# Attention kernel with three rotating max banks, masks of single-head diagonal tiles on VectorE, and the unit loop written out

## The reference

```python
Q, K, V = (split_heads(x @ W.T) for W in (Wq, Wk, Wv))      # [4, 16, 1024, 16]
Q, K = rope(Q), rope(K)
logits = einsum('bhnd,bhmd->bhnm', Q, K) / sqrt(16)
logits = where(causal, logits, -inf)
probs = softmax(logits, axis=-1)
attn = einsum('bhnm,bhmd->bhnd', probs, V)
```

## Time and profile before

| | us |
|---|---|
| median of 3 runs | 1235.57 |
| lowest and highest run | 1234.23, 1236.41 |
| the profiled execution's own time | 1237.32 |
| its span, first to last instruction | 1235.6 |
| TensorE matmul busy | 1099.6 (89%) |
| VectorE busy | 705.3 (57%) |
| ScalarE busy | 478.9 (39%) |
| GpSimd busy | 335.9 (27%) |

### The profile page before, as it was taken

One profiled execution on the slowest core, in us unless ns is written; L12 is line 12 of the kernel. 1 busy time (PEld: TensorE's weight loads), 2 busy tenths in 40 slices (PEclk: granted clock), 3 DMA queues, 4 the chain that ended last, 5 costly groups with the idle time before them and its releaser, 6 DMA issues. The chain is left out here.

```text
span 1235.6 us, 19774 instructions
## 1 busy us (share of the span) xinstructions
PE 1099.6 (89%) x5906; PEld 571.6 (46%) x5906; DVE 705.3 (57%) x1452; ACT 478.9 (39%) x719; POOL 335.9 (27%) x478
## 2 busy tenths in 40 slices
PE   8990899999999999999983699999997799999995
PEld 4550234444443444444422466666664455555553
DVE  5992878888888888888811344554453133333332
ACT  2441046666666666666671222222222122222221
POOL 2335022222222222222221122322335322322332
PEclk9995589999999999999997699999999799999998
DMA  7657334444455455455007322212012212222211
GB/s 263 148 135 152 51 57 61 80 93 80 64 93 89 60 93 94 60 94 94 10 14 216 104 60 61 64 58 69 35 36 80 78 54 64 61 66 66 65 62 39
DMA packets 78253, 99.76 MB, mean 81 GB/s; under 512 B 28048, under 2 KB 64400, under 8 KB 74864
## 3 DMA queue, kind: packets, MB, share of 16 engines
q1 hardware_dynamic: 67568, 74.41, 29.3%
q0 software_dynamic: 5712, 15.93, 3.5%
q10 hardware_dynamic: 4912, 8.66, 2.3%
HBM read 65.86 MB, written 32.70 MB: 80 GB/s over the span
## 5 line engine op out<-in xcount | busy, mean ns | idle before, releaser
L592 DVE TENSOR_REDUCE maxima<-max_ps 128x1 f32<-128x512 f32 (+3 forms) x608 | 384.7, 660 | 114.6 <-PE max_ps L448 61.4
L539 ACT ACTIVATE probs<-scores_ps 128x1024 f32<-128x1024 f32 (+3 forms) x384 | 290.4, 809 | 160.0 <-PE scores_ps L468 158.5
L444 PE MATMUL max_ps<-k_stack,q_stack 96*128 96x512 bf16 (+3 forms) x768 | 248.7, 346 | 43.4 <-DMA q_stack<-q_parts 32.8
L468 PE MATMUL scores_ps<-q_stack,k_stack 99*128 99x512 bf16 (+3 forms) x768 | 182.9, 327 | 2.0 <-ACT probs L539 1.8
L676 POOL TENSOR_SCALAR_AFFINE_SELECT probs<-probs 128x512 f32<-128x512 f32 x128 | 81.2, 635 | 374.4 <-ACT probs L539 374.4
L444 PEld LDWEIGHTS max_ps<-k_stack,q_stack 96*128 96x128 bf16 x768 | 74.7, 98 | 233.2 <-DVE maxima L592 174.0
L488 PE MATMUL out_ps<-probs,v_ones 128*32 128x512 f32 (+3 forms) x1536 | 164.0, 499 | 4.0 <-POOL probs L676 1.8
L1087 ACT ACTIVATE silu<-gate_ps 128x512 f32<-128x512 f32 x71 | 42.4, 597 | 253.2 <-PE gate_ps L980 145.1
L1235 DVE TENSOR_TENSOR hidden<-silu,up_ps 128x512 f32<-128x512 f32 x71 | 48.7, 686 | 160.4 <-PE up_ps L990 105.4
L448 PE MATMUL max_ps<-mask,ident_bf 128*128 128x128 bf16 x512 | 104.8, 229 | 0.0
L999 PE MATMUL down_ps<-v_then_down,hidden_t 128*128 x312 | 79.1, 397 | 10.5 <-issue 9.7
(11 more groups left out here) (142 smaller groups left out, 1178.7 us busy)
## 6 DMA issues: line engine op xcount, KB each, us to landing
k_stack<-k_parts SPq DMA_DIRECT2D x96, 128.0 KB, 4.5
q_stack<-q_parts SPq DMA_DIRECT2D x96, 128.0 KB, 7.5
q_parts<-parts SPq DMA_DIRECT2D x32, 192.0 KB, 3.2
k_parts<-parts SPq DMA_DIRECT2D x32, 192.0 KB, 3.1
rows_in<-expert_rows SPq DMA_DIRECT2D x39, 136.0 KB, 2.1
sums_in<-expert_sums SPq DMA_DIRECT2D x39, 128.0 KB, 2.0
x_t<-in_x_cols SPq DMA_DIRECT2D x8, 512.0 KB, 11.2
heads_rows<-heads_out SPq DMA_DIRECT2D x32, 128.0 KB, 3.6
```

Source lines behind the costliest of these rows:

```text
L444: last = nc.tensor.matmul(bank, q_stack[:ROWS, u.slot, h0 + k, t * P:(t + 1) * P], k_stack[:ROWS, u.slot, h0 + k, chunk * BLOCK:chunk * BL ...
L468: last = nc.tensor.matmul(scores_ps[:, pair, k, n0:], k_stack[:ROWS_MAX, u.slot, h, mt * P:(mt + 1) * P], q_stack[:ROWS_MAX, u.slot, h, c ...
L539: nc.scalar.activation(probs[:, s % RING, 2 * pair:2 * pair + 2, n0:], scores_ps[:, pair, :, n0:], ACT.Exp).then_inc(exp_done, 1)
L592: nc.vector.tensor_reduce(maxima[:, u.slot, chunk, h0:h0 + heads, t], max_ps[:, n % 2, :heads * keys].rearrange("p (h k) -> p h k", h=head ...
```

## The change

The four parts of it, all in the attention stage:

- `max_ps` gets a third bank, the one that was `turn_ps`. Pieces, output transposes and the transpose of the maxima all take their bank in turn from one list (`bank_plan`), and TensorE waits for whoever had the bank three turns before. VectorE's normalise moves from steps 3 and 7 to steps 2 and 6.
- In the 16 single-head diagonal pieces the mask matmul is left out. VectorE instead runs one instruction that adds a float32 mask of 512 columns (`mask_wide`, in SBUF) to the tile and takes the maximum, and that also writes the sum to a scratch tile in bfloat16. Before it VectorE waits for its own piece n-3 and issues an event instruction (`stand`). Pieces with two and four heads keep the mask matmuls.
- GpSimd makes `mask_wide` at the start of the stage, ahead of its other constants, and VectorE waits for it once.
- `each_unit` writes out all 16 units. All waits get constant values.

```diff
-def each_unit(eng, step):
-
-    for i in range(2):
-        step(Unit.number(i))
-    with eng.Fori(0, (UNITS - 4) // Unit.RING) as turn:
-        for k in range(2, 2 + Unit.RING):
-            step(Unit(turn * Unit.RING + k, k % Unit.RING, turn + k // Unit.RING))
-    for i in range(UNITS - 2, UNITS):
+def each_unit(step):
+
+    for i in range(UNITS):
         step(Unit.number(i))
...
+def bank_plan(pieces, places, early):
...
+    users = [("piece", 0, n) for n in range(len(pieces))]
+    users += [("piece", 1, n) for n in range(2)] + [("max", 0, 0)] + [("piece", 1, n) for n in range(2, early)]
+    for u in range(UNITS):
+        for s in range(len(places) // 3):
+            if s == 2 and u:
+                users.append(("out", u - 1, 1))
+            if s == 6:
+                users.append(("out", u, 0))
+            if s == 9 and u + 1 < UNITS:
+                users.append(("max", u + 1, 0))
+            of = u + (1 if s < OWN_STEPS else 2)
+            for slot in range(3 * s, 3 * s + 3):
+                users += [("piece", of, n) for n in places[slot] if of < UNITS]
+    users.append(("out", UNITS - 1, 1))
+    return {user: at for at, user in enumerate(users)}, users
...
+        mask_wide = b.sb("mask_wide", [P, BLOCK])
+        masked_out = b.sb("masked_out", [P, 6, BLOCK], BF16)
         scores_ps = b.ps("scores_ps", [P, 2, 2, BLOCK])
-        max_ps = b.ps("max_ps", [P, 2, BLOCK])
+        max_ps = b.ps("max_ps", [P, BANKS, BLOCK])
         out_ps = b.ps("out_ps", [P, BLOCK])
-        turn_ps = b.ps("turn_ps2", [P, BT, P])
+
+        def bank(kind, u, n):
+            return max_ps[:, turn_at[kind, u, n] % BANKS]
...
+            def bank_free(kind, u, n):
+
+                at = turn_at[kind, u, n] - BANKS
+                if at < 0:
+                    return
+                kind, u, n = users[at]
+                if kind == "piece":
+                    pe.wait_ge(piece_reduced, PIECES * u + n + 1)
+                elif kind == "max":
+                    pe.wait_ge(neg_copied, u + 1)
+                else:
+                    pe.wait_ge(normed, 2 * u + n + 1)
...
-                    wait(pe, piece_reduced, PIECES * u.i + n - 1)
+                    bank_free("piece", u.i, n)
                     for k in range(heads):
-                        bank = max_ps[:, n % 2, k * keys:(k + 1) * keys]
-                        diagonal = chunk == t // BT
-                        last = nc.tensor.matmul(bank, q_stack[:ROWS, u.slot, h0 + k, t * P:(t + 1) * P],
+                        part = bank("piece", u.i, n)[:, k * keys:(k + 1) * keys]
+                        diagonal = chunk == t // BT and heads > 1
+                        last = nc.tensor.matmul(part, q_stack[:ROWS, u.slot, h0 + k, t * P:(t + 1) * P],
...
                 pe.wait_ge(combined, u.i + 1)
-                wait(pe, normed, 2 * u.i - 1)
-                nc.tensor.transpose(turn_ps[:GROUP * SEQ_TILES, 0],
+                bank_free("max", u.i, 0)
+                nc.tensor.transpose(bank("max", u.i, 0)[:GROUP * SEQ_TILES, :P],
...
                 pe.wait_ge(out_copied, 2 * u.i + c + 1)
-                wait(pe, normed, 2 * u.i + c)
-                if c == 1:
-                    wait_neg = u.ahead(1)
-                    if wait_neg.exists():
-                        pe.wait_ge(neg_copied, wait_neg.i + 1)
+                bank_free("out", u.i, c)
...
                     dve.wait_ge(piece_done, PIECES * u.i + n + 1)
+                    if chunk == t // BT and heads == 1:
+                        wait(dve, piece_reduced, PIECES * u.i + n - 3)
+                        stand(dve, dve_stood)
+                        nc.vector.tensor_tensor_reduce(
+                            masked_out[:, n % 6, :keys], bank("piece", u.i, n)[:, :keys], mask_wide[:, BLOCK - keys:], 1.0,
+                            NEG, ALU.add, ALU.max, maxima[:, u.slot, chunk, h0:h0 + 1, t]).then_inc(piece_reduced, 1)
+                        continue
...
-                    if s == 3:
+                    if s == 2:
                         normalise(u.ahead(-1), 1)
-                    if s == 7:
+                    if s == 6:
                         normalise(u, 0)
...
+            dve.wait_ge(wide_made, 1)
             reduce(Unit.number(0), range(PIECES))
...
+            nc.gpsimd.memset(mask_wide[:], 0.0).then_inc(consts_half, 1)
+            pool.wait_ge(consts_half, 2)
+            tail = mask_wide[:, BLOCK - P:]
+            nc.gpsimd.affine_select(out=tail, in_=tail, compare_op=ALU.is_ge, fill=NEG, base=0,
+                                    pattern=[[-1, P]], channel_multiplier=1).then_inc(wide_made, 1)
```

More of the change, by code:

```diff
@@ L349, in attend @@
     STEPS, PIECES = len(steps), len(pieces)
+    BANKS = 3
+    turn_at, users = bank_plan(pieces, places, EARLY)
     DIAGONAL = [s for s, (c, mt, _) in enumerate(steps) if mt >= BT * c]
@@ L383, in attend @@
         heads_stored = [b.sem("heads_stored0"), b.sem("heads_stored1")]
-        pool_stood = b.sem("pool_stood")
+        pool_stood, dve_stood, wide_made = b.sem("pool_stood"), b.sem("dve_stood_a"), b.sem("wide_made")
         block = ctx.enter_context(nc.Block())
@@ L423, in _ @@
             send_neg(Unit.number(0))
-            each_unit(sp, step)
+            each_unit(step)
             store_heads(Unit.number(UNITS - 1), 1)
@@ L447, in find_max @@
                         if diagonal:
-                            last = nc.tensor.matmul(bank[:, keys - P:], ident_bf[:], mask[:],
+                            last = nc.tensor.matmul(part[:, keys - P:], ident_bf[:], mask[:],
                                                     start=False, stop=True)
@@ L495, in turn_out @@
                 pe.wait_ge(out_copied, 2 * u.i + c + 1)
-                wait(pe, normed, 2 * u.i + c)
-                if c == 1:
-                    wait_neg = u.ahead(1)
-                    if wait_neg.exists():
-                        pe.wait_ge(neg_copied, wait_neg.i + 1)
+                bank_free("out", u.i, c)
                 for t in range(BT):
-                    last = nc.tensor.transpose(turn_ps[:, t], out_t[:, c, t * P:(t + 1) * P], ident[:])
+                    last = nc.tensor.transpose(bank("out", u.i, c)[:, t * P:(t + 1) * P], out_t[:, c, t * P:(t + 1) * P], ident[:])
                 last.then_inc(out_turned, 1)
@@ L527, in _ @@
             pe.wait_ge(k_ones, 1)
-            each_unit(pe, step)
+            each_unit(step)
             times_v(Unit.number(UNITS - 1), STEPS - 1)
@@ L553, in negate @@
                 wait(act, neg_split, 4 * u.i)
-                nc.scalar.mul(neg_max[:], turn_ps[:GROUP * SEQ_TILES, 0], -1.0).then_inc(neg_copied, 1)
+                nc.scalar.mul(neg_max[:], bank("max", u.i, 0)[:GROUP * SEQ_TILES, :P], -1.0).then_inc(neg_copied, 1)
             def load_weights(u):
-                if isinstance(u.i, int) or u.slot == 1:
+                if not 2 <= u.i < UNITS - 2 or u.slot == 1:
                     return
@@ L578, in _ @@
             negate(Unit.number(0))
-            each_unit(act, step)
+            each_unit(step)
             copy_out(Unit.number(UNITS - 1), 1)
@@ L591, in reduce @@
                     dve.wait_ge(piece_done, PIECES * u.i + n + 1)
+                    if chunk == t // BT and heads == 1:
[5 more added lines that the diff above has]
+                        continue
                     nc.vector.tensor_reduce(maxima[:, u.slot, chunk, h0:h0 + heads, t],
-                                            max_ps[:, n % 2, :heads * keys].rearrange("p (h k) -> p h k", h=heads),
+                                            bank("piece", u.i, n)[:, :heads * keys].rearrange("p (h k) -> p h k", h=heads),
                                             X, ALU.max).then_inc(piece_reduced, 1)
@@ L609, in normalise @@
                 wait(dve, heads_stored[c], 16 * u.i)
-                rows = turn_ps[:].rearrange("p t (h e) -> p t h e", h=GROUP)
+                rows = bank("out", u.i, c).rearrange("p (t h e) -> p t h e", t=BT, h=GROUP)
                 nc.vector.reciprocal(recip[:, c], rows[:, :, :, DK]).then_inc(recip_done, 1)
@@ L630, in _ @@
             reduce(Unit.number(1), range(EARLY))
-            each_unit(dve, step)
+            each_unit(step)
             normalise(Unit.number(UNITS - 1), 1)
@@ L690, in _ @@
             split_neg(Unit.number(0))
-            each_unit(pool, step)
+            each_unit(step)
 def by_batch(eng, step):
```

## The result

The changed kernel takes 1184.4 us in the median of four runs (1182.9 to 1186.2), the one before 1235.3: a ratio of 0.9587 (95% interval 0.9572 to 0.9602). In a second series of runs it took 1187.2 us, against 1236.2 for the one before (ratio 0.9598, 0.9581 to 0.9615). So 49 to 51 us are gone, about 4.1%. The forecast was 37.5 off, 1198, with 1190 as its lower end: the direction and the place were right, the size was not.

What follows compares the result with a forecast made beforehand. TensorE was taken to bound the attention units, with stalls on two banks. 15 x (0.96 masks + 1.4 third bank) = 35.4, plus 0.6 loop and 1.5 start, gave 37.5 us off: 1198 us, range 1190 to 1225.

Steps and rivals of the forecast that it cites:

- What bounds it: Attention units: TensorE sets the 31.3 us period, 29.6 us streaming, switching or awaiting inputs plus 1.7 us waiting for banks.
- Mask matmuls: TensorE in attention units: leaving out 16 single-head mask matmuls of 0.06 us saves 0.96 us a unit.
- The new instruction: VectorE in attention units: 16 adds with a maximum raise its work from 23.2 to 25.6 us; TensorE stays the bound.
- x: Cost of VectorE's add with a maximum above a plain reduce: taken as 0.15 us, bounds 0.08 and 0.6.
- below 0.1 us of latency where it waits: VectorE's queue: assumed delay from the added event instruction and its wait when VectorE is not behind.
- The third bank: TensorE's bank waits in attention units: 1.7 us removed less 0.3 left for lateness, saving 1.4 us a unit.
- reserve for a late combine: End of each attention unit: 0.3 us held back because VectorE's combine could come up to 0.6 us later.
- The start: Before the first exp: 51 pieces gain 0.10 us each, 5.1, less 3.6 for 24 new instructions: 1.5 us saved.
- The loop: Attention unit loop written out: 12 units times 0.05 us, 0.6 us saved; jump-fetch stalls of microseconds dismissed.
- The sum: Whole kernel: 35.4 over 15 periods, 0.6 and 1.5 make 37.5 us off, 1198 us as a median.
- The signs: Expected attention traces: period 28.6 to 29.1 us, VectorE busy some 26.5, new instruction 0.68 to 0.85, reduces every 0.60.
- VectorE as the bound at x = 0.4: Rival in attention units: VectorE needs 30.1 us a unit, about 14 us off, 1222 us; chance 0.13.

Runs made afterwards that it cites:

- u_banks: Kernel before with the unit loop written out and three rotating banks, transposes included, but all 32 mask matmuls and plain reduces kept: 1199.5 us.
- u_masks: Kernel before with the unit loop written out and the 16 single-head masks added on VectorE, still two max banks and separate transpose bank: 1240.7 us.
- masks_wait_first: u_masks with VectorE's wait on its own third last piece and the event instruction moved ahead of the wait for the tile: 1227.0 us.
- fill_015: Kernel after with an 80-column reduce ahead of each new VectorE instruction, about 0.15 us more for each: 1201.2 us.
- loop_after: Kernel after with units 2 to 13 put back in the hardware loop on all engines: 1200.6 us.
- fill_040: Kernel after with a 320-column reduce ahead of each new VectorE instruction, about 0.40 us more for each: 1252.9 us.
- loop_vector_alone: Kernel after with units 2 to 13 in the hardware loop on VectorE only, all other engines written out: 1199.6 us.
- four_heads: Kernel after with the two four-head pieces of a unit also masked on VectorE, by an add into SBUF and then a reduce: 1181.2 us.

## Why the prediction was wrong

- **What bounds it** was right: TensorE streams in the attention units and stalls on two banks. My count of nine stalls and 1.7 us a unit was short: u_banks got 1.94 us a unit back.
- **Mask matmuls**, 0.96 us a unit: right (0.92), but only with the third bank. I added the parts as if each held alone. With two banks the part is a loss of 6 us (u_masks), or half its worth with the waits put first (masks_wait_first).
- **The new instruction**, x = 0.15: this term and what hung on it are the step that failed. It measured 0.01. My lower bound, 0.08, was a small instruction's price put on top; but the accumulator read of 0.08 us is recorded at the very start of the next instruction (228.42 and 229.03), so it does not push it back. The Trainium skill was right that there are two instructions ("VectorE: DVE Perf Modes", Two Vector instructions with no wait between them), and the trace shows both; it says nothing of a price, and there is nearly none. The term "below 0.1 us of latency where it waits" measured 0.17 (u_masks), hidden in the kernel after.
- **The third bank**, 1.4 us a unit: too low by 0.54, of which 0.24 is the count above and 0.3 the reserve for a late combine, which at the real x was not needed. At the x that I assumed the reserve itself was too small: fill_015, with x at about 0.16, loses 0.8 us a unit, and takes 1201.2 us, near the forecast of 1198, with the short reserve on one side and the short count and the start on the other.
- **The start**, 1.5 us: measured 6.8. The step of 0.10 us a piece was right (0.70 to 0.60); the 3.6 us taken off for x were nearly all not there (24 x 0.01 = 0.2). The rest: gaps between groups of reduces, 0.2 to 0.3 us each, were not in the sum and are mostly gone, and pieces of 384 columns, priced as 512, follow each other at 0.47 us where VectorE has no gap (126.21 to 126.68). So a piece fell by 0.13 us in the mean, not by 0.10.
- **The loop**, 0.6 us: right for the kernel before. My dismissal of the Trainium skill's rule on jumps ("Runtime: NRT & Kernel Launch", Instruction fetch mechanics: a taken branch whose target is not in the loaded pages waits for a fetch) was right for its rows and wrong for the change: with the masks on VectorE the loop would have cost three gaps of 4.7 to 5.8 us, and the trace agrees with the rule there, with a fetched packet in each gap. Writing it out is worth 13 to 16 us there (loop_after against the two series of the kernel after).
- **The sum.** 15 x 0.54 + 5.3 = 13.4 on top of 37.5 is 50.9, less 0.6 for the masks (0.92 in place of 0.96) 50.3; measured 49.0 to 49.7 in the spans. Of the 13.4, 7.9 hang on x (the reserve, 4.5, and 3.4 at the start): with x = 0.01 the prediction's own sum is 45.4 off, 1190, the very end of the range. The other 5.5, the short count of the bank waits (3.6) and the rest of the start (1.9), put the result outside it. The lower end was the sum at x = 0.08 with the counted stalls and 2 us for the last stage: its unknown price was bounded, though not low enough, its counts were not.
- **The signs.** Max tiles without waits for one another, 0.22 to 0.23 us from a tile of 512 columns to the next tile or scores, the new instruction at 0.69 us and unit 0's reduces every 0.60 came as said. The period, 28.37, and VectorE's 24.5 us a unit lie below the 28.6 to 29.1 and the 26.5 that were named, the one by the short count (31.3 - 0.96 - 1.94 is 28.4), the other by x.
- **The rivals.** The third bank does pay. VectorE as the bound at x = 0.4 was priced at 1222 and measured 1252.9 (fill_040): VectorE's work alone, plus 0.5, does not give the period, which is 2.6 us longer than that work. TensorE then waits 17.0 + 11.2 us in 12 units for the combine; how much of the 2.6 is that and how much the depth of three banks was not separated. The prediction's count of 264 new instructions is 8 too high, since 8 of the 24 at the start belong to unit 1, which is among the 15: the kernel has 256.

## What to carry to other kernels

The waits of a two-deep rotation are a cycle of latencies, so whatever takes work off one engine but starts later on the other can lose (here 6 us); deepen the rotation first, then move the work, and value each part with the other in place. Put waits that are always met, and event instructions, ahead of the wait that is not. Before an engine's stream is made longer inside a hardware loop, check that its turn of the loop still runs without a gap at the jump back; where the profile says "issue" for some microseconds once a turn, write that engine's stream out.

## What the hardware showed that was not expected

- In the loop of the kernel before VectorE's instruction stream stays loaded, and a unit with a jump back in it is no longer than the others (31.29 us in the mean, 31.24 written out). The longer stream of the kernel after stands 4.7 to 5.8 us at each jump, for VectorE alone (loop_after, loop_vector_alone), and is fetched again in every turn. How long a stream may be was not tried.
- An add with a maximum over 128x512 in PSUM and SBUF costs 0.61 us back to back, the plain reduce 0.60, accumulator read included.
- A wait already met and an event instruction, placed behind the wait for the tile, delay the start by 0.17 us (0.60 after the tile's start in u_masks, 0.43 in masks_wait_first).
- The same code of the last stage takes 560 to 570 us from one profiled execution to the next, more than some changes in the attention are worth. The mean granted clock in it was 0.95 in the shortest (four_heads) and 0.94 before and after; whether the clock explains all of it was not tried.
